# A two-layer decoder on one core: expert weights, convolution feed-forward and mask laid out anew

## What is computed

```python
# feed-forward of layer 0 (bit_linear rounds its input to 8 bits per token, its weights to -1, 0, 1)
h = bit_linear(x, w1)                               # 128 -> 512
h = conv1d(h over the sequence, conv_w, taps 3, padding 1) + conv_b   # depthwise
return bit_linear(silu(h), w2)                      # 512 -> 128

# masked cross attention of layer 1, 16 heads of 8
scores = where(mask == 0, -1e9, q @ k.T); attn = softmax(scores); out = (attn @ v) @ Wu + bu

# experts of layer 1
a, g = split(x @ w1[e], 2); y = (silu(a) * g) @ w2[e]      # for the expert e with the largest probability
out = y * max_prob
```

## Time and profile before

| | us |
|---|---|
| median of 3 runs | 1929.0 (1927.7 to 1929.32) |
| the profiled execution, its own time | 1931.2 |
| its span, first to last instruction | 1929.4 |
| PE busy | 1719.7 (89%) |
| DVE busy | 1387.2 (72%) |
| ACT busy | 1273.6 (66%) |
| POOL busy | 855.6 (44%) |

### The profile page before, as it was taken

One profiled execution on the slowest core, in us unless ns is written; L12 is line 12 of the kernel. 1 busy time (PEld: TensorE's weight loads), 2 busy tenths in 40 slices (PEclk: granted clock), 3 DMA queues, 4 the chain that ended last, 5 costly groups with the idle time before them and its releaser, 6 DMA issues. The chain is left out here.

```text
span 1929.4 us, 52384 instructions
## 1 busy us (share of the span) xinstructions
PE 1719.7 (89%) x13531; PEld 1481.4 (77%) x13531; DVE 1387.2 (72%) x4413; ACT 1273.6 (66%) x3518; POOL 855.6 (44%) x2194
## 2 busy tenths in 40 slices
PE   5777779999997999996999999799999999289997
PEld 3444458888886999995888888578888888288887
DVE  5777658778885888885888888578888888334443
ACT  4444368888885777775888888478888888122222
POOL 2222145555551222223555555256778777423333
PEclk9999869999998999997999999899999999699999
DMA  8950000000000000000000000000111111099996
GB/s 240 399 222 0 0 12 13 14 12 12 12 12 3 1 0 0 0 1 1 1 0 0 0 0 0 8 23 24 32 34 31 33 32 30 30 279 289 290 281 204
DMA packets 122074, 124.14 MB, mean 64 GB/s; under 512 B 35317, under 2 KB 100488, under 8 KB 122000
## 3 DMA queue, kind: packets, MB, share of 16 engines
q1 hardware_dynamic: 117392, 114.40, 18.8%
q0 software_dynamic: 4320, 8.53, 1.3%
q10 hardware_dynamic: 288, 0.34, 0.1%
HBM read 79.57 MB, written 44.12 MB: 64 GB/s over the span
## 5 line engine op out<-in xcount | busy, mean ns | idle before, releaser
L1036 PE MATMUL xa_ps_o<-xa_vb,xa_pt 128*128 128x96 f32 x2048 | 246.7, 274 | 0.0
L1036 PEld LDWEIGHTS xa_ps_o<-xa_vb,xa_pt 128*128 128x128 f32 x2048 | 239.5, 192 | 0.1
L881 ACT ACTIVATE xa_pt<-xa_ps_pt 128x512 f32<-128x512 f32 x256 | 139.1, 595 | 97.1 <-PE xa_ps_pt L955 97.1
L1203 PE MATMUL ffn_ps_h<-ffn_xdt,w1t 128*128 128x128 f32 x1536 | 184.6, 276 | 0.4 <-ACT ffn_xdt L1169 0.4
L693 DVE TENSOR_REDUCE xa_mx<-xa_ps_s 128x8 f32<-128x512 f32 x256 | 164.9, 686 | 24.8 <-PE xa_ps_s L971 21.2
L1203 PEld LDWEIGHTS ffn_ps_h<-ffn_xdt,w1t 128*128 128x128 f32 x1536 | 179.0, 194 | 0.7 <-ACT ffn_xdt L1169 0.7
L845 POOL TENSOR_TENSOR xa_km<-xa_kt,const_sb 128x256 f32<-128x256 f32 x256 | 152.5, 617 | 37.9 <-ACT xa_kt L894 28.6
L699 DVE TENSOR_TENSOR xa_pr<-xa_ps_s,xa_mx 128x512 f32<-128x512 f32 x256 | 163.6, 679 | 0.2
L971 PE MATMUL xa_ps_s<-xa_km,xa_qm 64*128 64x256 f32 x1024 | 149.9, 412 | 4.0 <-POOL xa_km L845 4.0
L875 ACT ACTIVATE xa_pr<-xa_pr 128x512 f32<-128x512 f32 x256 | 147.2, 622 | 3.6 <-DVE xa_pr L699 0.8
L955 PEld LDWEIGHTS xa_ps_pt<-const_sb,xa_pr 128*128 128x128 f32 x1024 | 111.0, 142 | 41.7 <-issue 41.7
(11 more groups left out here) (271 smaller groups left out, 4776.7 us busy)
## 6 DMA issues: line engine op xcount, KB each, us to landing
exp_w1b<-in_L_ffn_w_dram SPq DMA_DIRECT2D x71, 512.0 KB, 3.7
x_sorted<-no_row SPq DMA_DIRECT2D x1, 34320.0 KB, 91.2
exp_w2b<-in_L_ffn_w_dram SPq DMA_DIRECT2D x71, 256.0 KB, 4.1
xa_cn<-in_ctx_dram SPq DMA_DIRECT2D x128, 64.0 KB, 1.8
exp_xg<-x_sorted SPq DMA_DIRECT2D x71, 66.0 KB, 3.0
xa_mi<-in_mask_BxSxS_ik_dram SPq DMA_DIRECT2D x128, 32.0 KB, 2.1
out_dram<-exp_y,exp_token POOLq DMA_INDIRECT x71
x_sorted<-x_sb,place POOLq DMA_INDIRECT x64, 2.4
```

The lines of the kernel that those rows point to most:

```text
L881: nc.scalar.activation(pt[:, 512 * hf:512 * hf + 512], ps_pt[hf][:, :], ACT.Copy).then_inc(s["pt_sb"], 1)
L1036: last = nc.tensor.matmul(ps_o[:, 2 * VW * g:2 * VW * g + av_w], pt[:, P * g:P * g + P], vb[(r + 1) % RING][:, 2 * VW * g:2 * VW * g + av_ ...
L1203: last = nc.tensor.matmul(ps_h[c][:, 0:P], k.w1t[:, j, c, :], xdt[:, :, j:j + S], start=j == 0, stop=j == 2)
```

## The change

**Experts.** All down weights (2 MB) are loaded once into `w2e` by `load_weights`, ahead of the fill of `x_sorted`; `w2b` and its transfer are gone. PE reads the tile's owner into a register and takes the moving operand from `w2e` at a computed address. The up weights' transfer waits for `up_done` in place of `y_done`.

**Feed-forward.** The hidden tile is computed with tokens on the output partitions: the transposed tokens are stationary (three shifted copies of them, in a ring of four), 512 hidden units of `w1t` move, one matmul for each tap, and the bias is added by one bf16 matmul over 65 rows (the bias split in three bf16 parts in rows 0, 32 and 64 of `conv_rows`, all else zero). Silu is one instruction, and its result `g` in SBUF is read by L1095 and L1158; the four transposes back are gone. The normalisation moves from DVE to ACT, with a shift that POOL computes in two more small steps. The lead is 7. `prepare` splits the bias.

**Mask.** `twice` holds the 64-row identity twice side by side in each half of the partitions, and each half of PSUM gets its mask by a contraction of that half's 64 rows.

The raw weights' buffers are released after `prepare`. The core of the diff:

```diff
@@ load_weights
-        raw.load(sp, k.conv_b[:, :], a["L0_ffn_conv_b"].rearrange("(c p) -> p c", p=P))
+        raw.load(sp, raw.conv_b[:, :], a["L0_ffn_conv_b"].rearrange("(one h) -> one h", one=1).broadcast_to([BROWS, F]))
+    sp.dma_start(k.w2e[:, :].rearrange("p (e c n) -> p e c n", e=E, c=FC),
+                 a["L1_ffn_w2"].rearrange("e (c p) n -> p e c n", p=P)).then_inc(k.expert_weights, 16)
@@ prepare, vector
+                nc.vector.memset(k.conv_ones[:, :], 1.0)
+                after(nc.vector.memset(k.conv_rows[:, :], 0.0))
+                for i in range(3):
+                    row = slice(BSTEP * i, BSTEP * i + 1)
+                    nc.vector.tensor_copy(k.conv_rows[row, :], part[i][row, :])
+                    if i < 2:
+                        after(nc.vector.tensor_copy(rounded[:, :], part[i][:, :]))
+                        after(nc.vector.tensor_tensor(part[i + 1][:, :], part[i][:, :], rounded[:, :], ALU.subtract))
                 dve.wait_ge(s["total"], 1)
@@ softmax_attention, tensor
                             for hf in range(2):
-                                nc.tensor.matmul(ps_s[:, hf, :].rearrange("p (g c) -> p g c", g=4), k.identb[:, :],
-                                                 mb[:, :, :].rearrange("p b c -> p (b c)").unsqueeze(1).broadcast_to([P, 4, P]),
+                                rows = slice(HALF * hf, HALF * hf + HALF)
+                                nc.tensor.matmul(ps_s[:, hf, :].rearrange("p (g c) -> p g c", g=4),
+                                                 twice[rows, :, :].rearrange("p h c -> p (h c)"),
+                                                 mb[rows, :, :].rearrange("p b c -> p (b c)").unsqueeze(1).broadcast_to([S, 4, P]),
                                                  start=True, stop=False)
@@ bit_ffn, vector
-                    if live(t + 5):
-                        layernorm_scale(nc, dve, k, t + 5, ln, xn[:, :]).then_inc(ln["normed"], 1)
-                        dve.wait_ge(ln["normed"], t + 6)
-                        nc.vector.tensor_reduce(am[0][:, :], xn[:, :], axis=AX.X, op=ALU.max,
+                    if live(t + 6):
+                        dve.wait_ge(ln["normed"], t + 7)
+                        nc.vector.tensor_reduce(am[0][:, :], xn[r % 2][:, :], axis=AX.X, op=ALU.max,
                                                 apply_absolute_value=True).then_inc(s["am0"], 1)
-                pipeline(dve, nt, 5, body, unroll=4)
+                pipeline_ring(dve, nt, 7, body)
@@ bit_ffn, gpsimd
+                        pool.wait_ge(ln["rstd"], t + 8)
+                        nc.gpsimd.tensor_tensor(minus[:, 1:2], ln["mv"][:, 0:1], ln["r"][:, :], ALU.mult).then_inc(s["product"], 1)
+                        pool.wait_ge(s["product"], t + 8)
+                        nc.gpsimd.tensor_tensor(shift[:, :], minus[:, 0:1], minus[:, 1:2], ALU.mult).then_inc(s["shift"], 1)
@@ bit_ffn, scalar (body(t, r), after the copy of gq and the scaling into gr)
+                    if live(t + 7):
+                        act.wait_ge(s["shift"], t + 8)
+                        wait(act, s["xr"], t + 6)
+                        nc.scalar.activation(xn[(r + 1) % 2][:, :], k.x[:, col(t + 7), :].rearrange("p a d -> p (a d)"), ACT.Identity,
+                                             bias=shift[:, 0:1], scale=ln["r"][:, 0:1]).then_inc(ln["normed"], 1)
                     if live(t + 3):
-                        wait(act, s["gt_done"], t + 3)
-                        for c in range(FC):
-                            act.wait_ge(s["h_done"], FC * t + 3 * FC + 1 + c)
-                            nc.scalar.activation(g[:, c * P:(c + 1) * P], ps_h[c][:, 0:P], ACT.Silu,
-                                                 bias=k.conv_b[:, c:c + 1]).then_inc(s["g"], 1)
+                        act.wait_ge(s["h_done"], t + 4)
+                        wait(act, s["gr"], t + 3)
+                        nc.scalar.activation(g[:, :], ps_h[(r + 1) % 2][:, :], ACT.Silu).then_inc(s["g"], 1)
+                    if live(t + 6):
+                        act.wait_ge(s["xq"], t + 7)
+                        wait(act, s["xt_done"], t + 6)
+                        nc.scalar.activation(xd[:, :], xq[:, :], ACT.Copy, scale=step[0][:, 0:1]).then_inc(s["xd"], 1)
...
+                        tokens = ps_xt[:, 0:P].rearrange("p (b q) -> p b q", b=2)
+                        nc.scalar.activation(xdt[(r + 1) % RING][:, 1, :, :], tokens, ACT.Copy)
+                        nc.scalar.activation(xdt[(r + 1) % RING][:, 0, :, 1:S], tokens[:, :, 0:S - 1], ACT.Copy)
+                        nc.scalar.activation(xdt[(r + 1) % RING][:, 2, :, 0:S - 1], tokens[:, :, 1:S], ACT.Copy).then_inc(s["xt_sb"], 1)
@@ bit_ffn, tensor
-                        for c in range(FC):
-                            last = nc.tensor.transpose(ps_g[:, c * P:(c + 1) * P], g[:, c * P:(c + 1) * P], ident)
-                        last.then_inc(s["gt_done"], 1)
                     if live(t + 3):
                         pe.wait_ge(s["xt_sb"], t + 4)
-                        for c in range(FC):
-                            for j in range(3):
-                                last = nc.tensor.matmul(ps_h[c][:, 0:P], k.w1t[:, j, c, :], xdt[:, :, j:j + S],
-                                                        start=j == 0, stop=j == 2)
-                            last.then_inc(s["h_done"], 1)
+                        wait(pe, s["g"], t + 2)
+                        nc.tensor.matmul(ps_h[(r + 1) % 2][:, :], k.conv_ones[:, :], k.conv_rows[:, :], start=True, stop=False)
+                        for j in range(3):
+                            last = nc.tensor.matmul(ps_h[(r + 1) % 2][:, :], xdt[(r + 3) % RING][:, j, :, :].rearrange("p b q -> p (b q)"),
+                                                    k.w1t[:, j, :, :].rearrange("p c h -> p (c h)"),
+                                                    start=False, stop=j == 2)
+                        last.then_inc(s["h_done"], 1)
@@ experts, sync
-                        wait(sp, s["y_done"], t)
+                        wait(sp, s["up_done"], t)
                         sp.dma_start(w1b[q][:, :], w1[bass.ds(e, 1), :, :].rearrange("one d f -> d (one f)")
                                      ).then_inc(s[f"w_in{q}"], 16)
-                        sp.dma_start(w2b[q][:, :, :], w2[bass.ds(e, 1), :, :].rearrange("one (c p) n -> p (one c) n", p=P)
-                                     ).then_inc(s[f"w_in{q}"], 16)
@@ experts, tensor
+                    if live(t):
+                        e = pe.value_load(k.owner[0:1, col(t)], min_val=0, max_val=E - 1)
...
-                            last = nc.tensor.matmul(ps_y[q][:, 0:D], hg[q][:, c * P:(c + 1) * P], w2b[r % WRING][:, c, :],
+                            last = nc.tensor.matmul(ps_y[q][:, 0:D], hg[q][:, c * P:(c + 1) * P], k.w2e[:, bass.ds(e * (FC * D) + c * D, D)],
                                                     start=c == 0, stop=c == FC - 1)
```

More of the change, by code:

```diff
@@ L29 @@
 CONV_BANK = 3
+BSTEP = 32
+BROWS = 2 * BSTEP + 1
 E = 8
@@ L274, in prepare @@
         bvb = sb("bv_cols", [P, 2, P])
+        part = [raw.conv_b] + [sb(f"bias_part{i}", [BROWS, F]) for i in range(2)]
+        rounded = sb("bias_rounded", [BROWS, F], BF16)
         asum = sb("asum", [P, 2])
@@ L672, in _ @@
                 last.then_inc(s["consts"], 1)
+                if masked:
+                    for h2 in range(2):
+                        rows = slice(S * h2, S * h2 + S)
+                        nc.vector.tensor_copy(twice[rows, :, :], k.const[rows, C_ID + S * h2:C_ID + S * h2 + S].unsqueeze(1)
+                                              .broadcast_to([S, 2, S]))
                 if route:
@@ L1223, in experts @@
         w1b = [sb(f"w1b{i}", [P, 2 * F]) for i in range(WRING)]
-        w2b = [sb(f"w2b{i}", [P, FC, D]) for i in range(WRING)]
         xn = sb("xn", [P, D])
@@ L1422, in decoder @@
         if 6 in phases:
-            experts(nc, k, out, a["L1_ffn_w1"], a["L1_ffn_w2"])
+            experts(nc, k, out, a["L1_ffn_w1"])
         else:
```

104 lines of the change are left out of this document (54 added, 50 removed).

## The result

The changed kernel takes 1882.0 us (1881.6 to 1882.2, four runs) against 1928.4 for the kernel before in the same comparison (1927.5 to 1929.3, four runs): a ratio of 0.976, 95% interval 0.975 to 0.977. The forecast was 1884. The profiled execution of the changed kernel took 1881.6 us, its span is 1879.7.

What follows compares the result with a forecast made beforehand. Waits between nearly full engines bound the feed-forward, PE the masked attention, late weights the experts. Terms -14 - 10.5 - 24 + 3.5 = -45, from 1931.2 less 2.2 to the median, gave 1884 us, range 1866 to 1924.

Steps and rivals of the forecast that it cites:

- Feed-forward: -14 forecast: Feed-forward: 0.31 us saved a tile, -18 over 60 tiles, +4 for the deeper start; bounds -20 to +4.
- It and Silu are done by 2.1: Feed-forward, ACT: normalisation starts about 1.15 us after the scaling, following POOL's 1.52 us chain, and ends with Silu by 2.1.
- ACT's 3.50: Feed-forward: ACT's cycle from scaling to scaling takes 3.50 us after the change and ends last, setting the ordinary step.
- The second rival: Feed-forward: ACT or POOL sets the step, which stays at 3.79 us; 1902 us in all, chance 0.13.
- DVE's ring: Feed-forward: DVE's cycle from scaling to scaling, without the normalisation, takes 0.81 + 2.61 = 3.42 us.
- The deeper start, +4 forecast: Feed-forward: the pipeline is two tiles deeper, each start step costing 2.04 us, so +4 us.
- Mask: -10.5 forecast: Masked attention: the two 64-row mask passes overlap, saving 0.21 us a tile except where POOL starts it; bounds -13.5 to 0.
- Experts: -24 forecast: Experts: the 0.38 us a tile of waiting for weights mostly goes, 27 us less 3 for late landings; bounds -27 to -8.
- the lead of the sequencer: Experts: PE's sequencer works 1.9 us ahead, so the register load and computed addresses pass under queued matmuls and cost nothing.
- the first rival: Experts: PE's register load is not covered and each tile pays it; 1903 to 1942 us, chance 0.15.
- the 0.4 us of room: Experts: up weights arrive 5.2 us into the 5.6 available before their gate, in time with 0.4 to spare.
- Preparation: +3.5 forecast: Preparation: splitting the bias adds seven steps of 0.5 us to DVE's chain, +3.5 us; bounds 2.5 to 5.

Runs made afterwards that it cites:

- the kernel with both orders: Changed kernel with DVE's statistics under ACT's scaling, variance at the body's head, and ACT's three copies ahead of the dequantising: 1863.0 us.
- the fourth experiment: Changed kernel with DVE taking the feed-forward's variance ahead of the maximum of the hidden tile: 1881.7 us.
- the sixth: Changed kernel with only DVE's order altered (statistics under the scaling, variance at the body's head), ACT's copies left behind the dequantising: 1872.1 us.
- the eighth kernel: Changed kernel with the bias split on POOL instead of DVE and only the edge columns of the three copies zeroed: 1881.0 us.
- the third kernel: Changed kernel with the mask added by the full 128-row identity matmul again: 1893.8 us.
- the fourfold load: Changed kernel with PE reading the owner four times for each expert tile, three of them unused: 1956.6 us.
- The ninth experiment: Changed kernel with the down weights moved again for each tile into a ring that nothing reads or waits for: 1902.2 us.
- eleventh: Changed kernel with the up weights' transfer waiting for y_done again in place of up_done: 1883.8 us.

## Why the prediction was right

**Feed-forward: -14 forecast, -12.0 measured.** The mechanism held (normalisation, one Silu and three copies on ACT, no transposes back). The term of the ring that was mis-sized is POOL's chain, behind "It and Silu are done by 2.1". From the end of the variance to ACT's normalisation I counted 1.52 us; it is 704.09 - 702.28 = 1.81, because POOL's last step takes 0.41 in the median beside DVE's rounding, where it takes 0.19 in the kernel with both orders and does not meet the rounding, and because ACT starts 0.13 after its end (703.96). The variance itself ends 0.34 before the scaling, about where I had it (0.37). What I had not asked is behind what the variance stands on DVE: behind the maximum over the Silu that waits for this very chain. So its length goes round a ring, 1.81 to the normalisation, 0.40 to Silu, 0.64 to the maximum and 0.77 to the end of the variance: 3.62. With 1.52 in it, this ring would be 3.33 and hidden under ACT's 3.50. ACT's normalisation starts 1.47 after the scaling, not 1.15, the step is 3.62, not 3.50, and four tiles take 14.97, not 14.55 (before the change 15.87, not 15.8: behind a turn the step is 703.32 - 699.45 = 3.87). The second rival (ACT or POOL sets the step) is thus half true: POOL sets it, at 3.62 and not at 3.79. DVE's ring was priced too short as well, 3.42 against the 3.61 of the fourth experiment; ACT's 3.50 was about right (3.48 in the sixth).

The deeper start, +4 forecast, looks right at 3.4 by luck: the eighth kernel, with hardly any zeroing, comes to its first scaling 15.3 us after the stage's start against 12.5 before, so the two tiles cost 2.8, and the other 0.6 is the zeroing of the three copies, which I had not counted.

**Mask: -10.5 forecast, -13.1 in the stage, 11 to 12 by undoing it.** The overlap of the pair is as read from the scores. From first to last mask (the first of each pair) it is 385.3 us before and 371.4 after:

```profile
L965 PE MATMUL xa_ps_s<-xa_mb,identb x128: 376/379/634, 1250.8 to 1636.3; 128*128 128x512 bf16 x128
```

```profile
L987 PE MATMUL xa_ps_s<-xa_mb,xa_twice x128: 372/386/606, 1240.1 to 1611.5; 64*128 64x512 bf16 x128
```

In the third kernel, with the full-row mask put back, it is 383.0, so 2.3 of these 13.9 us are not the mask's: 1.9 of them lie in the first four tiles. Step by step, the mask's 11.6 us are unequal. Three masks of the changed kernel, one without a wait between two that waited for POOL:

```profile
1408.06 0.39 PE L987 MATMUL xa_ps_s<-xa_mb,xa_twice 64*128 64x512 bf16 x2 [0.69 <-POOL xa_km L866]
1413.63 0.39 PE L987 MATMUL xa_ps_s<-xa_mb,xa_twice 64*128 64x512 bf16 x2
1419.60 0.39 PE L987 MATMUL xa_ps_s<-xa_mb,xa_twice 64*128 64x512 bf16 x2 [0.37 <-POOL xa_km L866]
```

The steps are 5.57 and 5.97 us; the same two take 5.83 and 6.11 in the third kernel. Of the 63 steps, 31 end at a mask for which the changed kernel's trace names no wait for POOL. These gain 0.27 on average and 0.30 in the median, which is the whole of 0.52 less 0.22; I had counted 0.21, taking 0.1 to move ahead of the mask. The other 32 end at a mask that waited for POOL, and they gain 0.10 on average, many of them nothing. So counting nothing for the tiles that POOL starts was nearly right, but after the change they are half of the steps; in the kernel before they are 12, the fifth that I had read. A gain counted too small, for too many tiles: that the product came out near 11 is partly luck.

**Experts: -24 forecast, -25.2 measured.** The price of a tile was right, 3.17 to about 2.8 forecast, 3.19 to 2.84 measured, and the register load on PE is covered, as the lead of the sequencer said; the first rival is out, and the fourfold load shows how little is left (0.89 us a tile). The forecast's reasoning was loose in one place: it named the bytes, the issue and the transfer that lands last together, and it did not add up what SP needs for a tile. The ninth experiment separates the landing: without anyone waiting for it, 20 of the 25 us come back. Whether the bytes or the issue cost them stays open; SP's 3.07 us of work a tile in the kernel before, against PE's 2.79, speak for the issue. And the 0.4 us of room that I worked out for the up weights did no work: with the queues at 0.77 they come in time whichever wait SP has (eleventh).

**Preparation: +3.5 forecast and measured.** The added steps take 4.0 us, and 0.5 of that falls into a wait for the sums that DVE had before. Start: nothing, as forecast.

The sum of the misses is +2 in the feed-forward, -2.6 in the mask's stage (of which 1.7 stay when the mask is undone) and -1.2 in the experts; that they cancel to 2 us is luck, each being inside its own bounds.

## What to carry to other kernels

When a step's wait is removed, list the other closed rings through the same engines and their lengths before expecting the difference: here three rings lay within 0.14 us of each other (3.62, 3.61 and 3.48), shortening one gave nothing and shortening all of them gave 19 us. Ask of every instruction in a ring not only how long it takes but behind what it stands on its engine. And before a transfer is blamed for landing last, move its bytes without waiting for them, and add up what the engine that issues it needs for a turn: a late landing, full queues and an issuer without time to spare look alike in the list of releasers.

## What the runs showed of the hardware that I had not expected

A register load on PE takes 302 ns and 0.65 us of the sequencer with its register operations. While the sequencer's work for a tile stays under PE's 2.79 us it costs little (the second load 2.3 us over the stage's 71 tiles), and what goes beyond is paid in full (one, two and four loads: steps of 2.84, 2.88 and 3.90 us). POOL and DVE slow each other in both directions: DVE's scaling of 512 columns went from 0.49 to 1.23 us beside a subtraction on POOL, and POOL's product of one column from 0.19 to 0.41 in the median beside DVE's rounding, while DVE's steps kept their 0.43 beside ACT's casts. With rows, up weights and down weights in the queues, the DMA engines were busy 0.95 of the time at 294 GB/s, where the fill of the sorted rows alone moves 400. And SP needs 3.1 us of its own for two register loads and three issues a tile, which is more than the 25 matmul passes of PE take.
